# Causal attention whose score operands are loaded by column chunks: q and k sent out and stacked by 512 columns, from two engines, later stacks from GpSimd's queue

## What is computed

```python
q, k, v = heads(n @ Wq + bq), heads(n @ Wk + bk), heads(n @ Wv + bv)   # n = layernorm(x), 16 heads of width 8
att = softmax(where(tril, q @ k.T / sqrt(8), -inf))                   # 2048 x 2048 for each head
x = x + layernorm((att @ v) @ Wo + bo)
# then the second block: x = x + layernorm(six layers of local attention and feed-forward on layernorm(x))
```

## Time and profile before

| | us |
|---|---|
| median of three runs | 2617.71 (2608.78 to 2621.18) |
| the profiled execution | 2606.84, its span 2605.0 |
| front stage, to the first score matmul | 95.45 |
| first block's attention, first score matmul to last value matmul | 95.45 to 672 |
| second block begins, first weight matmul | 724.61 |
| PE busy | 2248.0 (86%) |
| DVE busy | 2042.2 (78%) |
| ACT busy | 1713.8 (66%) |

### The profile page before, as it was taken

The page is one execution under the profiler, slowest core; times in us unless marked ns, Lnnn a source line. Parts: engine busy times, 40 slices in busy tenths (PEclk is TensorE's granted clock), DMA queues, the critical chain, the costliest instruction groups (busy, mean ns, idle before and its releaser), DMA issues. The chain is left out here.

```text
span 2605.0 us, 93094 instructions
## 1 busy us (share of the span) xinstructions
PE 2248.0 (86%) x36506; PEld 1449.7 (56%) x36660; DVE 2042.2 (78%) x2644; ACT 1713.8 (66%) x3577; POOL 908.6 (35%) x502
## 2 busy tenths in 40 slices
PE   2158989899469999999989998999989999899994
PEld 1023333332237766767666666767667676676764
DVE  5248777674568888888878888888888888888884
ACT  1034566567357877777777777777767777777773
POOL 4100000000044545454444444444444444444440
PEclk8579999999789999999999999999999999999996
DMA  3410111100001112111121111211121111211110
GB/s 103 60 46 2 21 20 21 20 2 1 1 23 30 35 27 56 47 33 29 39 55 37 32 30 48 55 28 34 28 55 47 31 31 29 62 39 31 31 30 22
DMA packets 63521, 89.38 MB, mean 34 GB/s; under 512 B 20278, under 2 KB 31492, under 8 KB 63060
## 3 DMA queue, kind: packets, MB, share of 16 engines
q1 hardware_dynamic: 62470, 81.90, 13.9%
q0 software_dynamic: 608, 1.37, 0.2%
HBM read 28.48 MB, written 4.39 MB: 13 GB/s over the span
## 5 line engine op out<-in xcount | busy, mean ns | idle before, releaser
L668 POOL TENSOR_TENSOR arena<-arena 128x1024 f32<-128x1024 f32 x192 | 465.8, 2426 | 937.4 <-ACT arena L744 937.4
L719 ACT ACTIVATE arena<-bank 128x512 f32<-128x512 f32 (+3 forms) x640 | 316.9, 551 | 312.3 <-PE bank L912 162.4
L1210 DVE TENSOR_REDUCE arena<-bank 128x1 f32<-128x1024 f32 (+7 forms) x384 | 335.5, 908 | 178.0 <-PE bank L889 135.3
L985 PEld LDWEIGHTS bank<-ident,arena 128*128 128x128 f32 x3072 | 339.8, 142 | 184.2 <-issue 114.4
L769 ACT ACTIVATE arena<-bank 128x512 f32<-128x512 f32 x768 | 418.3, 603 | 23.5 <-PE bank L985 19.9
L985 PE MATMUL bank<-ident,arena 128*128 128x128 f32 x3072 | 419.9, 279 | 13.3 <-DVE arena L1320 8.3
L979 PE MATMUL bank<-wqk,arena 128*128 128x512 f32 x768 | 388.7, 630 | 28.8 <-issue 15.1
L685 POOL TENSOR_TENSOR arena<-arena 128x1024 f32<-128x1024 f32 x96 | 182.3, 1899 | 628.7 <-ACT arena L744 628.7
L744 ACT ACTIVATE arena<-bank 128x1024 f32<-128x1024 f32 x192 | 196.5, 1024 | 296.3 <-PE bank L979 293.4
L1307 DVE TENSOR_REDUCE arena<-arena 128x16 f32<-128x1024 f32 x192 | 233.4, 1216 | 144.2 <-POOL arena L674 140.2
L908 PE MATMUL bank<-arena 128*128 128x512 bf16 (+3 forms) x611 | 198.3, 363 | 63.5 <-DMA arena<-max_parts 54.0
(11 more groups left out here) (148 smaller groups left out, 3524.2 us busy)
## 6 DMA issues: line engine op xcount, KB each, us to landing
arena<-arena SPq DMA_DIRECT2D x768, 64.0 KB, 2.0
arena<-qk_parts SPq DMA_DIRECT2D x72, 128.0 KB
wqk<-in_L_ffn_Wqkv SPq DMA_DIRECT2D x12, 512.0 KB, 3.7
qk_parts<-arena SPq DMA_DIRECT2D x6, 512.0 KB, 2.6
wv<-in_L_ffn_Wqkv SPq DMA_DIRECT2D x6, 512.0 KB, 4.3
wo<-in_L_ffn_Wo SPq DMA_DIRECT2D x6, 512.0 KB, 4.0
w<-in_L_ffn_W SPq DMA_DIRECT2D x6, 341.0 KB, 3.2
out<-x SPq DMA_DIRECT2D x1, 1024.0 KB, 5.1
```

Of the source, the lines that this page charges most:

```text
L668: gp.tensor_tensor(rots[:, s], raw_qk[:, s], tab(l, t, s, 1).to_broadcast([P, H, DH]), ALU.mult).then_inc(done, 1)
L719: act.activation(ring[:, u % 8, lo:QC], bank[:, 4 + u % 3, lo:QC], ACT.Exp, scale=SCALE1).then_inc(exp_done, 1)
L985: last = pe.transpose(bank[:, out + b, P * (i % 4):P * (i % 4) + P], src[:, i].rearrange("p h d -> p (h d)"), ident[:, :])
L1210: ve.tensor_reduce(pmax[:, m, c:c + 1], src, AX.X, ALU.max).then_inc(piece_read, 1)
```

## The change

- q and k get a buffer each (`raw_q`, `raw_k`); PE, ACT and DVE go by block of 512 columns: q of block 0, k of block 0, q of block 1, and so on. DVE makes 24 casts and 16 subtractions of 512 columns in place of 6 and 4 of 2048.
- SP sends each block's six parts out by themselves (128 KB each, 24 DMAs), with a semaphore for each block.
- The stacks of group 0 are loaded in three chunks of columns, block 0, block 1, and blocks 2 and 3 together. SP issues the nine DMAs of q for a chunk, ACT the nine of k. PE waits for chunk 0 at its first maxima piece, for chunk 1 at unit 1, and for chunk 2 at unit 2.
- The zeros and ones of slot 0 go out ahead of the parts. The stacks of groups 1, 2 and 3 are issued by GpSimd, behind its tables; groups 2 and 3 wait for the last value matmul of the group two before.
- SP's maxima follow directly on group 0's stacks. The weights and biases come behind the last maxima.
- The planner's entry for slot 1 goes from 200 to 600 of its units. Group 1's items stand behind the 100 items of group 0 in any case, whose DVE costs alone are far above 600 units, so the list stays as it is.

```diff
+CHUNKS = ((0, 1), (1, 2), (2, 4))
-    ... stack_end = ... {0: 0, 1: 200}
+    ... stack_end = ... {0: 0, 1: 600}
-        raw = arena[:, 12288:14336]
+        raw_q, raw_k = arena[:, 12288:14336], arena[:, 4096:6144]
+        def stack(eng, g, slot, sides, lo, hi, done):
+            for s in sides:
+                dst = kst if s else qst
+                for i in range(3):
+                    for j in range(3):
+                        r = (3 * i + j) * D1
+                        part = qk_parts[s, j if s else i].rearrange("(g h d) t -> d g h t", g=NHG, h=HG)
+                        eng.dma_start(dst[r:r + D1, bass.ds(slot, 1), :, lo:hi], part[:, bass.ds(g, 1), :, lo:hi]).then_inc(done, 16)
...
 SP:
-            for s, p3 in ((0, parts_q), (1, parts_k)):
-                for i in range(3):
-                    sp.wait_ge(parts_ready, 3 * s + i + 1)
-                    sp.dma_start(qk_parts[s, i], p3[i]).then_inc(parts_out, 16)
-            sp.wait_ge(parts_out, 96)
+            def parts(b):
+                cols = slice(QC * b, QC * b + QC)
+                for s, p3 in ((0, parts_q), (1, parts_k)):
+                    for i in range(3):
+                        sp.wait_ge(parts_ready, 6 * b + 3 * s + i + 1)
+                        sp.dma_start(qk_parts[s, i, :, cols], p3[i][:, cols]).then_inc(parts_out[b], 16)
-            for s in range(2):
-                sp.wait_ge(stack_clear, 2 * (s + 1))
-                ... ones, stack(s, s)
-                sp.wait_ge(ones_in, 16 * (s + 1))
-                sp.wait_ge(stack_in, 16 * NSTACK * (s + 1))
+            sp.wait_ge(stack_clear, 2)
+            ones_row(sp, 0, first_in[0])
+            clear_maxima(sp, 0, first_in[0])
+            for c, (lo, hi) in enumerate(CHUNKS):
+                for b in range(lo, hi):
+                    parts(b)
+                for b in range(lo, hi):
+                    sp.wait_ge(parts_out[b], 96)
+                stack(sp, 0, 0, (0,), QC * lo, QC * hi, first_in[c])
+            for k, what, *i in order:
+                if what == "turn":
+                    maxima(k, k % 2, i[0])
             weights_qk(sp, 0)
             ...
             biases(sp)
-            for k, what, *i in order:
-                if what == "turn":
-                    maxima(k, k % 2, i[0])
-                elif what == "pv" and i[0] == NS - 1 and k + 2 < NHG:
-                    sp.wait_ge(pv_done, NS * (k + 1))
-                    stack(k + 2, k % 2)
 GpSimd:
-            gp.wait_ge(parts_out, 96)
+            for b in range(4):
+                gp.wait_ge(parts_out[b], 96)
             ... memsets on slot 1, tables
+            ones_row(gp, 1, ones_in)
+            for g in range(1, NHG):
+                if g >= 2:
+                    gp.wait_ge(pv_done, NS * (g - 1))
+                stack(gp, g, g % 2, (0, 1), 0, T, stack_in)
+                clear_maxima(gp, g % 2, stack_in)
 ACT:
-            for s in range(2):
-                if s:
-                    act.wait_ge(parts_ready, 3)
-                for b in range(4):
+            for b in range(4):
+                for s, raw in ((0, raw_q), (1, raw_k)):
                     ...
+            act.wait_ge(stack_clear, 2)
+            for c, (lo, hi) in enumerate(CHUNKS):
+                for b in range(lo, hi):
+                    act.wait_ge(parts_out[b], 96)
+                stack(act, 0, 0, (1,), QC * lo, QC * hi, first_in[c])
 PE:
+                if g == 0 and (h, t % 4, c) == (0, 0, 0):
+                    for n, (first, _) in enumerate(CHUNKS):
+                        if first == u:
+                            pe.wait_ge(first_in[n], 16 * (18 + 2 * (n == 0)))
 DVE:
-            for s, p3 in ((0, parts_q), (1, parts_k)):
-                ve.wait_ge(qk_read, 4 * (s + 1))
-                for i in range(3):
-                    ve.tensor_copy(p3[i], raw).then_inc(parts_ready, 1)
+            for b in range(4):
+                for s, raw, p3 in ((0, raw_q, parts_q), (1, raw_k, parts_k)):
+                    ve.wait_ge(qk_read, 2 * b + s + 1)
+                    ... the same three casts and two subtractions, on 512 columns
```

More of the change, by code:

```diff
@@ L363, in build @@
         pT_ready = sem("pT_ready")
-        parts_out = sem("parts_out")
+        parts_out = [sem(f"parts_out_{b}") for b in range(4)]
+        first_in = [sem(f"first_in_{c}") for c in range(len(CHUNKS))]
         parts_ready = sem("parts_ready")
@@ L518, in first_query, with clear_maxima, ones_row @@
             return P * max(0, kt - QC // P * qc) if qc else 0
+        def stack(eng, g, slot, sides, lo, hi, done):
[6 more added lines that the diff above has]
+                        eng.dma_start(dst[r:r + D1, bass.ds(slot, 1), :, lo:hi], part[:, bass.ds(g, 1), :, lo:hi]).then_inc(done, 16)
+        def clear_maxima(eng, slot, done):
+            eng.dma_start(qst[ROWS:ROWS + 3, bass.ds(slot, 1)],
+                          a["c_zeros"].rearrange("r (s h t) -> r s h t", s=1, h=HG)).then_inc(done, 16)
+        def ones_row(eng, slot, done):
+            eng.dma_start(kst[ROWS:ROWS + 3, slot], a["c_ones"].rearrange("r (h t) -> r h t", h=HG)).then_inc(done, 16)
         @block.sync
@@ L528, in _ @@
                 sp.dma_start(b_vo[:, i, :], a[f"L0_attn_b{n}"].partition_broadcast(P)).then_inc(w_in_in, 16)
-            for s, p3 in ((0, parts_q), (1, parts_k)):
-                for i in range(3):
-                    sp.wait_ge(parts_ready, 3 * s + i + 1)
-                    sp.dma_start(qk_parts[s, i], p3[i]).then_inc(parts_out, 16)
-            sp.wait_ge(parts_out, 96)
-            def stack(g, slot):
-                for i in range(3):
-                    for j in range(3):
-                        r = (3 * i + j) * D1
-                        for s, n, dst in ((0, i, qst), (1, j, kst)):
-                            src = qk_parts[s, n].rearrange("(g h d) t -> d g h t", g=NHG, h=HG)[:, bass.ds(g, 1)]
-                            sp.dma_start(dst[r:r + D1, bass.ds(slot, 1)], src).then_inc(stack_in, 16)
-                sp.dma_start(qst[ROWS:ROWS + 3, bass.ds(slot, 1)],
-                             a["c_zeros"].rearrange("r (s h t) -> r s h t", s=1, h=HG)).then_inc(stack_in, 16)
+            def parts(b):
[4 more added lines that the diff above has]
+                        sp.dma_start(qk_parts[s, i, :, cols], p3[i][:, cols]).then_inc(parts_out[b], 16)
             def maxima(g, slot, u):
@@ L556, in maxima @@
                              unit.rearrange("g i (h t) q -> i g h (t q)", h=HG)).then_inc(max_in, 16)
-            for s in range(2):
-                sp.wait_ge(stack_clear, 2 * (s + 1))
-                sp.dma_start(kst[ROWS:ROWS + 3, s], a["c_ones"].rearrange("r (h t) -> r h t", h=HG)).then_inc(ones_in, 16)
-                stack(s, s)
-                sp.wait_ge(ones_in, 16 * (s + 1))
-                sp.wait_ge(stack_in, 16 * NSTACK * (s + 1))
+            sp.wait_ge(stack_clear, 2)
[10 more added lines that the diff above has]
+                    maxima(k, k % 2, i[0])
             weights_qk(sp, 0)
@@ L858, in _ @@
             pe.wait_ge(w_in_in, 128)
-            for s in range(2):
-                for b in range(4):
-                    pe.wait_ge(xnT_read, b + 1)
+            for b in range(4):
+                pe.wait_ge(xnT_read, b + 1)
+                for s in range(2):
                     mm(bank[:, 4 - 4 * s + b, :], w_in[:, s, :], xnT[:, 512 * b:512 * b + 512],
@@ L864, in _ @@
             for t in range(NT):
[L865 removed]
+                pe.wait_ge(qk_read, 2 * (t // 4) + 1)
                 last = mm(bank[:, 4 + t // 4, P * (t % 4):P * (t % 4) + P], xnT[:, P * t:P * t + P], w_in[:, 2, :],
@@ L1183, in _ @@
             ve.tensor_copy(pattern8[:, :, :], pattern[:, :].unsqueeze(1).to_broadcast([P, 8, 2 * W])).then_inc(pattern_ready, 1)
-            for s, p3 in ((0, parts_q), (1, parts_k)):
-                ve.wait_ge(qk_read, 4 * (s + 1))
-                for i in range(3):
-                    ve.tensor_copy(p3[i], raw).then_inc(parts_ready, 1)
-                    if i < 2:
-                        ve.wait_ge(parts_ready, 3 * s + i + 1)
-                        step(ve.tensor_tensor(raw, raw, p3[i], ALU.subtract))
+            for b in range(4):
+                cols = slice(QC * b, QC * b + QC)
+                for s, raw, p3 in ((0, raw_q, parts_q), (1, raw_k, parts_k)):
+                    ve.wait_ge(qk_read, 2 * b + s + 1)
+                    for i in range(3):
+                        ve.tensor_copy(p3[i][:, cols], raw[:, cols]).then_inc(parts_ready, 1)
+                        if i < 2:
+                            ve.wait_ge(parts_ready, 6 * b + 3 * s + i + 1)
+                            step(ve.tensor_tensor(raw[:, cols], raw[:, cols], p3[i][:, cols], ALU.subtract))
             ve.wait_ge(w_in_in, 128)
```

13 lines of the change are left out of this document (6 added, 7 removed).

## The result

| | before | changed | |
|---|---|---|---|
| median, same chip | 2618.2 us (4 runs) | 2539.5 us (4 runs) | ratio 0.9698, 95% interval 0.9677 to 0.9719 |
| forecast | | 2550 (2518 to 2580) | 68 us gained; measured 78.7 |
| profiled execution | 2606.8 | 2540.6 | 66.3 us apart |

What follows compares the result with a forecast made beforehand. In the first 400 us one queue's order and slow stacks, with maxima queued behind them, were taken as the bound. 58.6 - 4 + 12.9 = 67.5, say 68 us, off 2617.7 gives 2550 us, range 2518 to 2580.

Steps and rivals of the forecast that it cites:

- The bound, and the chain: First 400 us: one queue's order and slow stacks bound the kernel; PE's remaining wait for unit 0's maxima is 27 us.
- Splitting: DVE's split of q and k by block: 2.45 us for three casts and two subtractions; PE can start at about 51.
- Chunks 0 and 1 and the parts behind them: Group 0's stack: chunk 0 in at 46.8, chunk 1 at 61.7; parts behind them take 3 and 5.4 us more.
- Chunk 2 at 60 GB/s: Group 0's last chunk: bytes set the price; issued at 67.1, it takes 1.2 + 21.4 us and is in at 89.7.
- Does the second engine help: Group 0's stack issued by SP and ACT: no gain except shorter issue; all transfers stay at 40 us.
- First score piece: PE's first score piece, after unit 0's maxima: at 95 in place of 153.6, including 2 us for meeting GpSimd's stack; gain 58.6.
- Unit 1's maxima: Their trip under GpSimd's stack of group 1: up to 5.6 us longer, none if they don't meet; 4 us taken as lost.
- The later stacks: Groups 2 and 3 on GpSimd's queue: maxima no longer stand behind a stack, so 4.2 + 8.7 = 12.9 us of waits go.
- Weights: Weights moved behind the last maxima: nothing waits for them, nothing gained on PE's side; their 12 us ahead is in the 58.6.
- The whole: Sum of the terms over the whole kernel: 58.6 - 4 + 12.9 = 67.5, say 68 us gained, 2550 against the median.
- Faster stacks: Rival for group 0's stack: two queues halve chunk times, score piece at about 73, gain 89 us, 2529; chance 0.15.
- GpSimd's queue is the bound: Rival: GpSimd's descriptor making delays group 1's stack; at five times SP's 40 us, 2651, slower than before; chance 0.04.

Runs made afterwards that it cites:

- the order runs: Changed kernel with SP alone issuing group 0's stack: one chunk, q first, 2550.4 us; three chunks, q and k pairs alternating, 2532.7 us.
- SP alone: Changed kernel with all 18 DMAs of each group 0 chunk issued by SP, q then k, none by ACT: 2539.1 us, ratio 0.9711.
- a kernel equal up to there: Changed kernel, but GpSimd waits for unit 1's maxima to be back before issuing group 1's stack: 2536.0 us, ratio 0.9691.
- the run with the order alone: Kernel before, front unchanged, with later stacks on GpSimd's queue and weights behind the last maxima: 2593.9 us, ratio 0.9906.
- ACT reversed: Changed kernel with ACT's nine k DMAs of each chunk in reversed order; chunk 2's rate showed three valleys: 2532.0 us, ratio 0.9671.

## Why the prediction was right, and where its sizes were off

**The bound, and the chain.** Right: one queue's order. A single wait for max_parts took the place of the 41.1 us, and it was the next thing late, at 8.3 us, not the 27 I gave, since the maxima were back 11 us sooner and PE came to it at 75.3 and not at 68. Three of PE's 7 us are its later start, and 3.7 are a wait for DVE at 70.64, behind the cast that took 2.42 us beside GpSimd's memsets; before, PE's wait there was 0.72.

**Splitting.** 2.45 us for three casts and two subtractions measured 2.7 (0.43 and 0.69 for an instruction of 512 columns, where I had 0.31 and 0.57 plus a share). PE could start at 54.04, not 51, later than the 53 I gave the kernel before's own split. These 3 us cost nothing, since chunk 2 ended later still.

**Chunks 0 and 1 and the parts behind them.** Forecast 34.9 / 49.8 / 67.1 for the three issues, measured 36.35 / 47.00 / 61.34. The term that was mis-sized is the parts' passage behind a chunk, 3 us and 5.4 us: it hardly adds to the chunk. From chunk 0's issue to chunk 1's took 10.7 us where I had 14.9, and from chunk 1's to chunk 2's 14.3 where I had 17.3. As I read it, the DMA engines that the chunk leaves idle carry their share of the parts meanwhile; no run tests that (156 GB/s from 47 to 61 us against 63 in chunk 2):

```profile
47.00:61.00 14.00, 5.82 (x27) 2.18 (x28) 11.70 (x26) 0.00 (x0) 0.00 (x0) 0.50 0.66 156
62.00:81.00 19.00, 6.95 (x26) 2.31 (x24) 12.76 (x17) 1.28 (x1) 18.79 (x21) 0.50 0.49 63
```

**Chunk 2 at 60 GB/s.** Right in number, 63, and half of the engines busy as in the earlier trace rows. The reason that I gave first, q and k of a pair on the same partitions at the same time, is what the order runs and the valleys bear out; that bytes set the price and not packets holds too, with 1.19 MB in 18 us as against some 40 had each packet its old price. But I priced the chunk as if the rate belonged to stacks as such. It belongs to this order, and not firmly: the same two queues made 66 and 89 in other runs, and SP alone, all q first, 85 and 132. That 63 stood so near the forecast 60 is in part luck. "Does the second engine help" has the answer no; whether it costs anything stays open. The Trainium skill's rule (DMA: Bandwidth & Descriptors, "Issuing engines are not separate DMA queues") is that starting DMAs from several engines saves sequencer time only; the traces agree in that two queues carried no more than one.

**First score piece.** Forecast 95, measured 83.6, 81.1 and, in a kernel equal up to there, 77.5. 5.8 of the 11.4 us are the earlier issue of chunk 2, 2 are the meeting with GpSimd's stack, which started at 86 behind the trip, 2.9 are chunk 2's own (19.7 us from its issue to the read back's, for 22.6), and 0.7 the way from there to PE.

**Unit 1's maxima.** Forecast 4 lost, with 5.6 as the most; measured 5.9 to 6.4, 7.2 longer from issue to read back. That the meeting is the cause is shown by the run without it, 1.94 us for the trip. My bound of ten packets at 0.56 us was too low; GpSimd's stack kept all 16 DMA engines busy and not eight, which it left out, but how packets queue there no run shows.

**The later stacks.** Forecast 12.9 won, measured 5.6 + 10.0 = 15.6, and the reason I gave doesn't carry it. I credited the move to another queue. The run with the order alone makes that move and wins nothing there: its trips took 25.0 and 23.7 us, beyond the 22 us of room. The order inside the stack brought them down to 10.1 and 12.9 us, and I had not priced it. That this term came out right is luck. The 2.7 us above the forecast may be the lower TensorE clock behind each stall (PE's granted clock was 0.69 from 469 to 480 us in the kernel before and 0.84 from 340 to 350), which I had not added; no run separates it.

**Weights.** The step was right in saying that nothing waits for them at the end. That their price ahead of the maxima was 12 us was the step of my sum that the runs refute, without harm to the total: in the changed kernel's place it is 31.

**The whole.** 70.0 - 6.4 + 15.6 = 79.2 by the traces' markers, 78.7 by the medians, against 58.6 - 4 + 12.9 = 67.5. The difference is 11.4 from the first score piece and 2.7 from the later stacks, less 2.4 at unit 1. The sum was also made on the profiled execution: 2539 there, 2540.6 measured, which looks better than it is, since the second block differed by 12.8 us between the two. Against the median, which was the forecast, it is 10 low.

**The rivals.** "Faster stacks" at 89 us did not happen in the changed kernel, but two kernels came to the first score piece near the 73 of that rival: SP alone at 73.8, without a second queue, and ACT reversed at 73.6, where the two queues did write different partitions for most pairs. "GpSimd's queue is the bound" had nothing for it: 18 stack DMAs were issued in 9.6 us and moved in 21, twice as fast as SP's. What GpSimd did cost is on the other side, DVE's cast under its memsets.

## What to carry to other kernels

Read a DMA queue as an engine with an order of its own: ask of every small transfer on which an engine waits what stands ahead of it, and note that a full queue also holds up the engine that issues. Neighbouring transfers, in one queue or in two, should write different partitions: on GpSimd's queue nine of q and then nine of k ran at 118 to 121 GB/s where the same eighteen in pairs ran at 67 to 76. Where an effect rests on one trace, take a second: the rate of one chunk with the same instructions was 132 and then 85 GB/s. And compare equal instructions of two traces, marker by marker, before the totals: here that split 79 us into four terms and set aside 13 us that belong to the second block.

## What the runs showed of the hardware that I had not expected

- Sixteen DMA engines, all busy, moved 118 to 121 GB/s in one order of transfers and 67 to 76 in another. A DMA share is no measure of rate.
- SP's issue of the DMA of w1 took 1.17 us on a free queue and 16.23 behind chunk 2.
- A 16 x 128 cast on DVE took 0.21 us alone, and 2.42 and 8.65 in two kernels in which it ended together with GpSimd's memsets on SBUF. Moving these memsets out from under unit 0's maxima wasn't tried.
- The second block, with the same instructions, took 1808 to 1826 us, on the whole longer where more 50 us stretches lay below full TensorE clock (six in the trace of 1810 us, twelve in that of 1826).
